# Three f16 products of split sums for the last head's own projection, and one addition moved to ScalarE and GpSimd

## What is computed

```python
z = layernorm(xn, ln1_g, ln1_b)
qkv = z @ w_in.T + b_in
q, k, v = split(qkv, 3);  k = q                    # 16 heads of 16
attn = softmax(einsum('nhld,nhsd->nhls', q, k) / 4)
out = einsum('nhls,nhsd->nhld', attn, v)           # heads side by side again
attention = out @ w_out.T + b_out
h = gelu(xn @ ternary(W1).T + b1)
ffn = h @ ternary(W2).T + b2
```

## Time and profile before

| | before |
|---|---|
| median of 3 runs | 1382.27 us (1381.38 to 1382.33) |
| the profiled execution | 1382.0 us, its span 1379.8 us |
| TensorE busy | 1359.6 us (99%) |
| VectorE busy | 1311.3 us (95%) |
| ScalarE busy | 1244.9 us (90%) |
| GpSimd busy | 230.6 us (17%) |
| the chain that ended last | DVE 81%, PE 15%, rest 4% |
| its largest part | maxima of VectorE, L988, 79% |

### The profile page before, as it was taken

How to read it: one execution, slowest core, us unless ns; L and a number is a source line. 1 busy time by engine, 2 the same in 40 slices (tenths; PEclk the granted TensorE clock), 3 DMA queues, 4 the chain that set the end, 5 groups by cost and what they waited for, 6 DMA issues and landing times.

```text
span 1379.8 us, 32101 instructions
## 1 busy us (share of the span) xinstructions
PE 1359.6 (99%) x13296; PEld 460.9 (33%) x13296; DVE 1311.3 (95%) x1350; ACT 1244.9 (90%) x2268; POOL 230.6 (17%) x385
## 2 busy tenths in 40 slices
PE   9899999999999999999999999999999999999999
PEld 6566642222222222222222222222222222222244
DVE  7888899999999999999999999999999999999935
ACT  7575569999999999999999999999999999999975
POOL 3212162000000000000000003333200225501200
PEclk9999999999999999999999999999999999999999
DMA  5333300000010001111010111000001112202122
GB/s 226 73 86 72 92 18 24 26 26 30 31 33 33 33 33 33 34 33 33 33 34 33 33 33 36 31 31 31 28 29 40 56 58 66 64 32 65 41 88 101
DMA packets 55724, 66.71 MB, mean 48 GB/s; under 512 B 33329, under 2 KB 38865, under 8 KB 55324
## 3 DMA queue, kind: packets, MB, share of 16 engines
q1 hardware_dynamic: 55146, 63.55, 14.7%
q10 hardware_dynamic: 434, 1.13, 0.2%
HBM read 40.77 MB, written 16.77 MB: 42 GB/s over the span
## 4 chain that ended last, share of the span: by engine, by line
DVE 81%; PE 15%; issue 1%; DMA 1%; ACT 1%; POOL 0%; SPq 0%; DVEq 0%
DVE part_max L988 79%; PE ps L1336 3%; PE ps L1245 3%; PE ps L1265 2%; PE ps L504 2%; PE ps L485 1%; PE ps L383 1%; PE ps L474 1%; DMA max_rows<-max_split 1%; PE ps L1358 0%; DVE w L980 0%; PE ps L514 0%; DMA x_parts<-weight_scratch 0%; PE ps L413 0%; DMA qry<-max_rows 0%
## 5 line engine op out<-in xcount | busy, mean ns | idle before, releaser
L988 DVE TENSOR_REDUCE part_max<-ps 128x1 f32<-128x1024 f32 x1024 | 1160.5, 1295 | 3.4 <-PE ps L383 3.4
L1220 ACT ACTIVATE w<-ps 128x512 f32<-128x512 f32 x2048 | 1109.4, 596 | 51.3 <-PE ps L474 16.3
L413 PE MATMUL ps<-w,v_ones 128*32 128x256 f32 (+1 forms) x7688 | 627.1, 398 | 0.3
L427 PE MATMUL ps<-qry,key 50*128 50x512 f16 x1984 | 398.9, 386 | 8.0 <-ACT w L1220 7.5
L383 PE MATMUL ps<-qry,key 48*128 48x512 f16 x2048 | 393.3, 380 | 0.7 <-DVE part_max L988 0.7
L413 PEld LDWEIGHTS ps<-w,v_ones 128*32 128x32 f32 x7688 | 151.3, 108 | 313.3 <-issue 160.2
L427 PEld LDWEIGHTS ps<-qry,key 50*128 50x128 f16 x1984 | 98.2, 92 | 430.0 <-ACT w L1220 412.3
L751 POOL COPY v_ones<-v_all 128x128 f32<-128x128 f32 x64 | 18.5, 291 | 689.0 <-PE ps L413 689.0
L383 PEld LDWEIGHTS ps<-qry,key 48*128 48x128 f16 x2048 | 100.0, 93 | 76.2 <-issue 16.0
L1336 PE MATMUL ps<-x_parts,w_ternary 128*128 128x512 f16 x256 | 62.0, 380 | 0.9 <-ACT hidden L1177 0.9
L1177 ACT ACTIVATE hidden<-ps,columns 128x512 f32<-128x512 f32 x64 | 41.2, 677 | 20.0 <-PE ps L1336 19.7
(11 more groups left out here) (169 smaller groups left out, 534.3 us busy)
## 6 DMA issues: line engine op xcount, KB each, us to landing
key<-q_parts SPq DMA_DIRECT2D x62, 128.0 KB
qry<-q_parts SPq DMA_DIRECT2D x62, 128.0 KB
o_heads<-o_evacuated SPq DMA_DIRECT2D x31, 256.0 KB, 9.9
key<-q_parts SPq DMA_DIRECT2D x66, 64.0 KB
qry<-q_parts SPq DMA_DIRECT2D x66, 64.0 KB
resid<-in_x SPq DMA_DIRECT2D x8, 512.0 KB, 7.7
q_parts<-q_split SPq DMA_DIRECT2D x16, 256.0 KB, 2.5
out<-resid SPq DMA_DIRECT2D x7, 512.0 KB, 4.0
```

The source lines that it names most:

```text
L413: mm = eng.matmul(pv[32 * c:32 * c + 2 * D, c0:c1], vst[:, kb, :], prob[kb % 2][:, c * BANK + c0:c * BANK + c1], start=(kb == 0), stop=(kb ...
L427: eng.matmul(ring_bank(v, i, False), key[v][r:r + KROWS, kb * P:(kb + 1) * P], qry[v][r:r + KROWS, c * BANK:(c + 1) * BANK], start=True, s ...
L988: dve.tensor_reduce(part_max[h % 2][:, blk, side:side + 1], pa[a % 2], AX.X, ALU.max).then_inc(s_r, 1)
L1220: act.activation(prob[kb % 2][:, c * BANK:(c + 1) * BANK], ring_bank(k, i, last), ACT.Exp, scale=exp_scale).then_inc(s_e, 1)
```

## The change

- `wl` becomes two f16 parts of the weights; four of its eight loads now copy from `wop` in on-chip memory, four copy a constant 1.0 from on-chip memory. Their place in SyncE's queue moves from behind the key pads to behind group 1, and they wait for `s_op`.
- The last head's values are scaled by 2^-9 and its column of ones is 2^6, both set by GpSimd.
- ScalarE evacuates to f16 (first part), VectorE subtracts it from PSUM for a second f16 part (`second_last`): after turns 4, 8 and 12 for 512 columns, at the end in two halves.
- The f32 product becomes three f16 products; the third waits for the second part (`s_lo`).
- Behind each reciprocal VectorE has a tensor_scalar that takes the scales out; at the end four reciprocals share one, and four additions follow.
- The last `add_y` is taken from VectorE: ScalarE copies the projection scaled from PSUM, GpSimd adds it.

```diff
+VLAST = 2.0 ** -9
+DLAST = 2.0 ** 6
...
-        wl = sb("wo_last", [P, C + 1])
+        wl = sb("wo_last_parts", [P, 2, C + 2], F16)
+        unit16 = sb("unit_f16", [1, 2], F16)
...
             if k0 == 0 and c:
                 eng.wait_ge(s_o, h + c - 1)
+                wait(eng, s_lo, c - 1)
...
-            eng.matmul(pl[m][:, 0:C + 1], o_last[c % 2][:, t * P:(t + 1) * P], wl[:, :], start=True, stop=True).then_inc(s_yl, 1)
+            first, second = (o_last[c % 2][:, i, t * P:(t + 1) * P] for i in range(2))
+            eng.matmul(pl[m][:, 0:C + 1], first, wl[:, 0, 0:C + 1], start=True, stop=False)
+            eng.matmul(pl[m][:, 0:C], first, wl[:, 1, 0:C], start=False, stop=False)
+            eng.wait_ge(s_lo, c + 1 if c < NCH - 1 or t < 2 else c + 2)
+            eng.matmul(pl[m][:, 0:C + 1], second, wl[:, 0, 0:C + 1], start=False, stop=True).then_inc(s_yl, 1)
...
             for g in range(1, HALF_GROUPS):
                 group(g)
+            sp.wait_ge(s_wz, 1)
+            sp.wait_ge(s_op, 1)
+            for j in range(NCH):
...
             sp.wait_ge(s_qs, 16 * KC * HALF_GROUPS)
             load_columns(0, 0, 0, L // 2, s_lh)
...
+                if h == NH - 1:
+                    pool.memset(vst[:, k0:k0 + NBLK // 2, D:2 * D], DLAST)
+                    pool.tensor_scalar(vst[:, k0:k0 + NBLK // 2, 0:D],
+                                       v_all[:, ds(b * NBLK + k0, NBLK // 2), ds(hh * D, D)], VLAST, None, ALU.mult).then_inc(s_vs, 1)
+                    return
...
+            pool.tensor_tensor(last_y, last_y, y_copy.rearrange("p (t c) -> p t c", c=C), ALU.add).then_inc(s_yd, 1)
...
+            def second_last(c, cols):
+                dve.wait_ge(s_o, NH + c)
+                dve.tensor_tensor(o_last[c % 2][:, 1, cols], pv_last[c % 2][:, cols], o_last[c % 2][:, 0, cols],
+                                  ALU.subtract).then_inc(s_lo, 1)
...
+            for n in range(2):
+                second_last(NCH - 1, slice(n * HALF, (n + 1) * HALF))
+            m0 = NBLK - TG
+            for m in range(m0, NBLK):
+                dve.wait_ge(s_yl, m + 1)
+                last = dve.reciprocal(d_last[:, m:m + 1], pl[m][:, C:C + 1])
...
+            for m in range(m0, NBLK):
+                add_row(m, NBLK - 1 if m < NBLK - 2 else NBLK)
...
+            act.activation(y_copy, py, ACT.Copy, scale=yun[:, 0:1]).then_inc(s_yc, 1)
```

More of the change, by code:

```diff
@@ L161, in attention_ffn @@
         below_sb = sb("below_half", [P, 4, BANK])
-        wl = sb("wo_last", [P, C + 1])
+        wl = sb("wo_last_parts", [P, 2, C + 2], F16)
+        unit16 = sb("unit_f16", [1, 2], F16)
+        d_last = sb("recip_of_den", [P, NBLK])
         r_last = sb("recip_last", [P, NBLK])
@@ L217, in attention_ffn @@
         on_rest = [scr[0:HR, n, :].bitcast(F16).rearrange("p (s n) -> p s n", s=2) for n in range(NCH)]
-        o_last = [qp[:, k, :, :].rearrange("p s n -> p (s n)").bitcast(F32) for k in range(2)]
+        o_last = [qp[:, k, :, :] for k in range(2)]
+        y_copy = o_sb[:, :]
         def o_parts(g, k):
@@ L339, in attention_ffn @@
         s_lr = sem("last_recip")
+        s_lo = sem("o_last_second_parts")
+        s_yc = sem("y_of_last_copied")
         s_ld2 = sem("y_last_added")
@@ L565, in _ @@
                 sp.dma_start(k[r:r + 2, :], key[0][ROWS:KROWS, :]).then_inc(s_pad, 16)
[L567 to L571, removed]
             def store_q(g):
@@ L623, in _ @@
                 group(g)
+            sp.wait_ge(s_wz, 1)
+            sp.wait_ge(s_op, 1)
+            for j in range(NCH):
+                sp.dma_start(wl[32 * j:32 * j + D, :, 0:C], wop[P - D:P, :, KC - 1, :]).then_inc(s_wl, 16)
+                sp.dma_start(wl[32 * j + D:32 * j + D + 1, 0, C:C + 2], unit16[:, :]).then_inc(s_wl, 16)
             sp.wait_ge(s_qs, 16 * KC * HALF_GROUPS)
@@ L697, in _ @@
                 pool.wait_ge(s_pc, n + 1)
-            pool.memset(wl[:, :], 0.0).then_inc(s_wz, 1)
+            pool.memset(unit16[:, :], 1.0)
+            pool.memset(wl[:, :, :], 0.0).then_inc(s_wz, 1)
             def rsqrt(g):
@@ L806, in _ @@
                     normalise(PAIR_IN[h - 1])
+            pool.wait_ge(s_yc, 1)
+            last_y = resid[:, NT - 2:NT, :]
+            pool.wait_ge(s_xb, NG)
+            pool.tensor_tensor(last_y, last_y, y_copy.rearrange("p (t c) -> p t c", c=C), ALU.add).then_inc(s_yd, 1)
         @block.vector
@@ L1058, in add_last, with add_row @@
                 dve.wait_ge(s_yl, m + 1)
-                dve.reciprocal(r_last[:, m:m + 1], pl[m][:, C:C + 1]).then_inc(s_lr, 1)
-                dve.wait_ge(s_lr, m + 1)
+                dve.reciprocal(d_last[:, m:m + 1], pl[m][:, C:C + 1]).then_inc(s_lr, 1)
+                dve.wait_ge(s_lr, 2 * m + 1)
+                dve.tensor_scalar(r_last[:, m:m + 1], d_last[:, m:m + 1], yun[:, 0:1], DLAST / VLAST, ALU.mult, ALU.mult).then_inc(s_lr, 1)
+                dve.wait_ge(s_lr, 2 * m + 2)
+                add_row(m, adds)
+            def add_row(m, adds):
                 dve.wait_ge(s_yd, adds)
@@ L1064, in add_last @@
                                          op0=ALU.mult, op1=ALU.add).then_inc(s_ld2, 1)
+            def second_last(c, cols):
+                dve.wait_ge(s_o, NH + c)
+                dve.tensor_tensor(o_last[c % 2][:, 1, cols], pv_last[c % 2][:, cols], o_last[c % 2][:, 0, cols],
+                                  ALU.subtract).then_inc(s_lo, 1)
             lasts = 0
[L1067 to L1071, removed]
+            for n in range(NBLK - 1):
                 add_y(n, lasts)
@@ L1077, in _ @@
                     normalise_rest(n - REST_AT)
[L1078 to L1083, removed]
+                for m in last_at(n):
+                    add_last(m, n + 1)
+                    lasts += 1
+                if n and n % TG == 0:
+                    second_last(n // TG - 1, slice(0, BANK))
+            for m in last_at(NBLK - 1) + last_at(NBLK)[:1]:
+                add_last(m, NBLK - 1)
+            for n in range(2):
[4 more added lines that the diff above has]
+                last = dve.reciprocal(d_last[:, m:m + 1], pl[m][:, C:C + 1])
+            last.then_inc(s_lr, 1)
+            dve.wait_ge(s_lr, 2 * m0 + 1)
+            dve.tensor_scalar(r_last[:, m0:NBLK], d_last[:, m0:NBLK], yun[:, 0:1], DLAST / VLAST, ALU.mult, ALU.mult).then_inc(s_lr, 1)
+            dve.wait_ge(s_lr, 2 * m0 + 2)
+            for m in range(m0, NBLK):
+                add_row(m, NBLK - 1 if m < NBLK - 2 else NBLK)
         @block.scalar
@@ L1211, in evacuate_last @@
                 wait(act, s_yl, TG * (c - 1))
-                act.activation(o_last[c % 2], pv_last[c % 2], ACT.Copy).then_inc(s_o, 1)
+                act.activation(o_last[c % 2][:, 0, :], pv_last[c % 2], ACT.Copy).then_inc(s_o, 1)
             def head(h, k, first=False, last=False):
@@ L1233, in _ @@
             evacuate_last(TG - 1)
+            act.wait_ge(s_y, NBLK)
+            act.wait_ge(s_os, 16 * (NH - 1))
+            act.activation(y_copy, py, ACT.Copy, scale=yun[:, 0:1]).then_inc(s_yc, 1)
         @block.tensor
```

## The result

The changed kernel takes 1393.81 us (median of 5 runs, 1392.99 to 1394.22), the kernel before beside it 1381.68 (5 runs, 1380.97 to 1382.33). The ratio is 1.0088, 95% interval 1.0077 to 1.0099: slower by 12 us. The forecast was 1391.5 within 1387.0 to 1394.0, so sign and range held, and the size was 2.3 us short. The profiled execution after has a span of 1392.0 us and a mean granted clock of 0.994, against 1379.8 and 1.000 before.

What follows compares the result with a forecast made beforehand. TensorE was taken to bound the kernel up to VectorE's long run of maxima and again in the last head. 7.0 + 2.0 - 0.15 + 0.7 = 9.5 us on 1382.0 gave 1391.5 us, range 1387.0 to 1394.0.

Steps and rivals of the forecast that it cites:

- the arithmetic at +0.55 in sum: Last head: -0.15 us for its projection turns and +0.7 us for the program's end.
- Part 1: SyncE's moved weight loads delay head 0's columns; TensorE stalls 7.0 us at its first score product.
- eight issues: SyncE issuing the eight moved loads ahead of the columns: 0.63 us each, 5.0 in all, bounds 4.4 and 5.2.
- landing after the last issue: Head 0's columns arrive 3.4 us after their last issue, read from DMA traffic, values 3.1 to 3.8.
- some tenths: Possible extra stall from transposes of x sharing the DMA engines with the columns' last bytes; not in the sum.
- the bound of 7.6: Upper bound in us of TensorE's stall at the first score product, with issues 5.2 and landing 3.8.
- Part 2: TensorE's clock falls to half rate after standing still at the first score product, costing 2.0 us.
- the rival with a steady clock: TensorE's clock stays at 2.4 GHz after the stall; stall and end remain: 1389.5 us, chance 0.28.
- The bound of 3.4: Upper bound in us of the clock's cost behind the stall: half of 6.8; lower bound nothing.
- Part 3: Last head's own projection: TensorE gains, VectorE's turns 6 to 9 lose; sum -0.15 us, bounds -1.3 and +1.2.
- Part 4: Program's end: subtractions, third products, tensor_scalar and four additions in a row put the last addition 0.7 us later.
- The rival that TensorE's stall would come out of slack before the long run of maxima: Slack at 166 to 204 us takes TensorE's 7 us back: 1382.5 us, chance 0.04.

Runs made afterwards that it cites:

- The loads late alone: Changed kernel with the eight weight loads and their waits moved behind head 4's steps in SyncE's queue: 1382.45 us, ratio 1.0006.
- the place alone: Kernel before with its own eight f32 loads moved ahead of head 0's columns, behind the same wait for wo's second part: 1390.6 us, ratio 1.0066.
- the wait alone: Changed kernel with the eight loads at head 4 but the wait for `s_op` kept ahead of the column loads: 1386.06 us, ratio 1.0039.
- the transposes held: Changed kernel with SyncE waiting for the first columns' landing before issuing group 3's transposes of x: 1391.42 us, one run.
- the matmuls put into the rest: Changed kernel with 34 matmuls on a constant, result unused, ahead of TensorE's wait for the column loads: 1390.98 us, ratio 1.0068.
- The reorder: Changed kernel, eight loads at head 4, VectorE doing the last head's row block ahead of `normalise_rest` in turns 6 to 9: 1380.76 us, ratio 0.9995.
- the omitted tensor_scalar: Changed kernel, eight loads at head 4, without the tensor_scalar behind each reciprocal, result not scaled back: 1383.49 us, one run.
- all three edits together: Changed kernel, loads at head 4, row block ahead of `normalise_rest`, scale folded into column 256's constant, each end reciprocal followed by its addition: 1380.40 us, ratio 0.9992.

## Why the prediction was right, and where it was short

**Which edit counts.** The prediction put the whole loss into the place of the eight loads, and counted the arithmetic at +0.55 in sum. The loads late alone show +1.3 in the medians (+0.9 in the means), with an interval that includes no change; the place alone, in the kernel before, shows +9.4. Right.

**Part 1, the stall: 7.0 forecast, 8.9 measured.** Each term against the trace:

| term | forecast | after |
|---|---|---|
| TensorE's arrival behind the queue's resumption | 68.84 - 63.3 = 5.54 | 67.77 - 62.16 = 5.61 |
| eight issues | 5.0 | 67.76 - 62.16 = 5.60 |
| column issues | 4.06 | 3.98 |
| landing after the last issue | 3.4 | 76.68 - 71.74 = 4.94 |
| stall | 7.0 | 8.91 |

The step that was mis-sized most is the landing. I read it from the DMA traffic, that is, from when the bytes stop flowing, and took the middle of two batches. Where an engine waits for it, it is 4.3, 4.4 and 4.4 us (the place alone, the wait alone, the transposes held) and 4.9 in the changed kernel: 0.9 to 1.5 more than my value. Two things were missing. The release comes later than the last byte, by 0.6 us in the one trace that shows both (the transposes held). And the traffic itself differs between runs: in finer stretches it ends 3.3 us after the last issue in the first batch of before, 4.0 in the second, where I had read 3.8, and 3.8 and 4.2 with the transposes held and with the loads late. The transposes, which the prediction named with "some tenths" and left out of the sum, may have a part in the 4.9; that isn't shown. The second error is the issues, 0.70 us each and not 0.63: the loads of two parts (16x2x256) take 0.64 to 0.74 and a new one starts every 0.70, while the copies I had taken the price from go at 0.65 a piece. Both terms lie outside the bounds that I gave them (5.2 and 3.8), so the bound of 7.6 for the stall was too narrow.

The fixed cost of about 2 us in the Trainium skill, "DMA: Bandwidth & Descriptors", section "Anatomy of one DMA", would have led further off: the landing of these transfers is 4.3 to 5.4 us behind the last issue. The page tells it of DMAs from another engine than SyncE.

**Part 2, the clock: 2.0 forecast, 2.7 measured.** The fall came, as the likelier of two cases, and the rival with a steady clock (1389.5) fell. The products from 76.68 to 82.73 took 6.05 us where they took 3.35, and the matmuls put into the rest give back 2.7 to 2.8. The bound of 3.4 holds. The 2.0 us stood for 4 us of work at half rate; here it was 6. The price isn't fixed: with the transposes held the work at half clock lasted under 4 us and cost 5.01 - 3.35 = 1.7. The rule of the Trainium skill, "TensorE: Matmul & The Clock Gate", section "What's actually happening", that an idle array is gated to half rate, is what the trace shows: 0.50 from 72 to 82 us, after a rest that began at 67.8. In the rests of 2.00 us and 2.75 us (the wait alone) the clock stayed.

**Part 3, the turns: the sum right to a tenth.** Forecast 17.9 us for five turns from turn 6, and measured:

```profile
1352.65 0.75 DVE L1067 SCALAR_TENSOR_TENSOR resid<-ps,y_unscale,resid 128x512 f32<-128x512 f32 x1 [1.69 <-PE ps L512]
...
1362.98 0.68 DVE L1096 TENSOR_TENSOR q_split<-ps,q_split 128x512 f16<-128x512 f32 x1
1363.58 0.74 DVE L1067 SCALAR_TENSOR_TENSOR resid<-ps,y_unscale,resid 128x512 f32<-128x512 f32 x1
...
1370.58 0.75 DVE L1067 SCALAR_TENSOR_TENSOR resid<-ps,y_unscale,resid 128x512 f32<-128x512 f32 x1 [1.90 <-PE ps L512]
```

1370.58 - 1352.65 = 17.93 against 17.28. TensorE's record of the third product in turn 9 shows the subtraction holding it, 0.40 us behind the second product, where it is 0.11 in other turns:

```profile
1363.32 0.27 PE L524 MATMUL ps<-wo_last_parts,q_split 128*128 128x256 f16 x1
1363.72 0.28 PE L526 MATMUL ps<-wo_last_parts,q_split 128*128 128x257 f16 x1
```

The sum is better than its parts. A turn of VectorE with `normalise_rest` was to take 3.69 us and takes 3.51, and the single steps of the forecast (3.7, 3.3, 3.7, 3.9 and 3.3) are off by 0.2 to 0.4 each (3.51, 3.52, 3.90, 3.50 and 3.50) and cancel; to that extent the tenth is luck. Outside these, a turn with its own product takes 3.28 instead of 3.40. From the first key product to the last `pv_block` the last head went from 52.20 to 52.07 us: -0.13, forecast -0.15. The reorder and the omitted tensor_scalar then showed both causes at work: 1.5 us go with the order, and 0.75 with the extra step while the order stays. The two don't add up, since with the right order the extra step costs nothing. The f16 products are a gain of 0.11 each that the change spent on VectorE's side.

**Part 4, the end: 0.7 forecast, 1.2 measured.** The end of the program on VectorE, after (the answer to the earlier trace rows):

```profile
1385.39 0.76 DVE L1096 TENSOR_TENSOR q_split<-ps,q_split 128x256 f16<-128x256 f32 x2 [0.21 <-ACT q_split L1254]
...
1387.19 0.17 DVE L1119 RECIPROCAL recip_of_den<-ps 128x1 f32<-128x1 f32 x1 [0.16 <-PE ps L526]
1387.39 0.23 DVE L1122 TENSOR_SCALAR recip_last<-recip_of_den,y_unscale 128x4 f32<-128x4 f32 x1
1387.82 1.66 DVE L1091 SCALAR_TENSOR_TENSOR resid<-ps,recip_last,resid 128x256 f32<-128x256 f32 x4 [0.20 <-DVE recip_last L1122]
```

The last addition starts at 1387.82 + 1.66 - 0.48 = 1389.0, that is 5.4 us behind the last `pv_block` against 4.5: +0.86. The 0.15 above the forecast lie in small waits between these steps. The prediction stopped at the last addition; from it to the end of the span it is 3.0 us and no longer 2.7, another 0.3, for which the sum had no term. The additions are 0.40 apart now and were 0.60, and the stores of their rows follow on SyncE. That these queue up is at most a part of it: with all three edits together the additions are about 0.60 apart again, and from the last one to the end it is 1377.7 - 1374.8 = 2.9 us. The cause stays open. GpSimd's addition was covered, as forecast, but its cover is thin: where the tensor_scalar was left out it came last by 0.28.

**Taken back?** The rival that TensorE's stall would come out of slack before the long run of maxima fell: the shift at 204 us is that at 83 us to 0.1.

The sum as it should have been: 8.9 + 2.7 - 0.13 + 1.2 = 12.7 on the profiled 1382.0 us, which makes 1394.7. The measured 1393.81 is lower because this execution was 1.1 us earlier ahead of the change and had 0.4 us less outside its span, and 0.7 came on in the middle. So three terms (landing with issues, clock, end) were all too small, and that the time lies within the stated range, 0.2 below its upper end, owes something to luck: one of the five runs, 1394.22, lies above it.

## What to carry to other kernels

Before small DMAs are moved in a queue, look at what stands behind them and how much the waiting engine has in hand there: eight small copies, of 16 KB at most, cost 8.9 us of TensorE because they and their wait stood ahead of one load that was needed. Read the landing of a transfer from an engine that waits for it, and where none does, add the time between the last byte and the release to what the traffic shows. When a product gets cheaper on TensorE and its operand dearer on VectorE, look at the order on VectorE first: freeing the bank before other work was worth 1.5 us in five turns, and made the extra step free in them.

## What the runs showed of the hardware

- Eight column loads, four of 64 KB and four of 32 KB: the waiting engine goes on 4.4 us after the start of the last issue with no other traffic. With a transposition issued 1.2 us behind it was 4.4 too, and with one 0.5 us behind 4.3 (the place alone), 4.9 (after) and 5.4 (with TensorE kept at work; 77.38 against 72.02). The second transposition itself takes 3.0 to 4.1 us on the queue in these four runs, instead of 1.8 to 2.1.
- From the end of the traffic to the release it is 0.6 us (75.4 to 76.0, the transposes held).
- A small copy (16x2x256 or 1x2x1) occupies SyncE's queue for 0.62 to 0.74 us whatever its size; weights loaded from memory (16x256) take 0.35 to 0.38 a piece.
- The granted clock fell to 0.50 in rests of 7.0, 8.4 and 8.9 us, each time while TensorE stood still, and work at half clock followed for 3.7 to 6 us. In rests of 2.0 and 2.75 us it stayed, the latter in the one run that has a trace.
